# Packing q and k in four pieces with x loaded earlier; in the layers, ScalarE norms the rows and their transposes move behind the k projection

## The chip, the cores and the metric

The kernel runs on one core of a Trainium2 chip. The metric is the device time of one execution in microseconds (us), the median of several runs. Names used below: PE is TensorE, ACT is ScalarE, DVE is VectorE, POOL is GpSimd and SP is the engine that issues the DMAs.

## The reference

Two stages, on 16 sequences of 512 rows with 256 channels, in float32:

```
# stage 1: attention with 16 heads of 16 channels, softmax over the HEADS, then a layernorm
scores = einsum('bqnd,bknd->bnqk', q, k) / sqrt(D)
attn = softmax(scores, axis=1)
x = layernorm(x + (attn @ v) @ Wo.T + bo)
# stage 2: two layers over the same rows
h = shift_token(x)                  # the second half of the channels comes from the row before
q, k = l2norm(q) * qs, l2norm(k) * ks; rotary; local attention with windows of 128 rows, 8 heads of 64
x = x + o @ wo
h = layernorm(shift_token(x)) * lg + lb
a, g = split(h @ w1 + b1)
x = x + (a * gelu(g)) @ w2 + b2
# and a last layernorm(x + ...)
```

## The kernel before

The kernel is written engine by engine: each engine has its own program, in the order of the code, and semaphores join them. Nothing reorders it; an instruction that waits holds back all that stands behind it on its engine.

**Stage 1** (`head_attention`) takes a sequence in 16 units `u` (4 query tiles by 4 key tiles). A unit on PE: subtract the maximum over the heads from the scores `S` (L504), sum the heads' exponentials (L535), the next unit's 16 score matmuls (L494, `scores_bank`), probabilities times v (L521). DVE takes the maximum over the heads (L371) once per unit, so its start times mark the units. Beside this, the projections of the next sequence are spread over the units by `QK_AT`; the float32 q and k are split into three bfloat16 parts (`parts`, ACT L296), and for each of the four pieces (q channels 0 to 127, q 128 to 255, k likewise) the last part is there two units after `READY_AT` = (2, 5, 8, 10), that is at units 4, 7, 10 and 12. SP then copies the parts from 128 partitions into `qk8`, where 8 combinations of parts (`TERMS`) lie in 8 groups of 16 partitions (`pack`, L200). Each transfer writes one group of 16 partitions. Before, q is packed at unit 7 and k at unit 12, 8 transfers of 256 KB each; the first score matmul of the next sequence, at the end of unit 15, waits until both have landed. A loop runs two sequences per round; the first sequence and the last ones are written out. x of the next sequence is loaded (`load_x`) when this one begins, behind its first transposes.

**Stage 2** (`layers`) takes 128 tiles `T` of 128 rows (2 layers, 16 sequences, 4 tiles `w_` each). While tile T is attended, tile T+1 is projected, tile T-1 gets its output projection, tile T-2 its layernorm, and the rows of one or two sequences before go through the feed-forward part. On PE a tile is, in order: transposes of q and k (L1460, L1464), hidden part 0 (L1435), `transpose_h` (x of T+1, L1342, and the normed rows `hn` of T-2, L1346, into the two halves of PSUM bank `X[2]`), times v (L1409), scores (L1380, L1389), transposes of the attention output (L1478), q projection (L1364), output projection (L1487), k projection, transposed probabilities of the first four heads (L1398), hidden part 1, scores of the other heads, times v, v projection, hidden part 2, w2 (L1514), transposed probabilities of the other heads. The w2 matmuls of a tile with even `w_` wait for a product on DVE (`gated`, L839 and L841), which waits for the gelu on ACT (L1095), which ACT does once per two tiles, in the tile with even `w_`, behind the evacuation of the first transposed probabilities (L1129). DVE norms the rows of T-2 at the start of a tile (L1222, L1224), ahead of the low parts of q and k.

Of the kernel before, what the change touches and what calls it, by code (L numbers as in the profile page):

```python
# [682 lines left out]
def layers(nc, ctx, x_a, x_b, y_out, w, W, raw, consts):  # L683
# [322 lines left out]
    def _(act):  # L1006
        def evacuate_hT(T, n, w_, layer):

            act.wait_ge(s_hT, T + 2)
            if tile_exists(T + 1):  # L1010
                p = (w_ + 1) % 2
                nc.scalar.activation(hT0[p][:, HIGH], X[2][:, 0:P], ACT.Copy)
                nc.scalar.activation(hT1[p][:, HIGH, 1:P + 1], X[2][:, P:2 * P], ACT.Copy)

                last_col = zero_col[:] if (w_ + 1) % TILES == TILES - 1 else X[2][:, 2 * P - 1:2 * P]
                last = nc.scalar.activation(hT1[1 - p][:, HIGH, 0:1], last_col, ACT.Copy)
            if tile_exists(T - 2):
                n2, w2_ = back(n, w_, 2)
# [572 lines left out]
```

## Time and profile before

| | us |
|---|---|
| median of 3 runs | 4712.84 (4704.44 to 4716.74) |
| the profiled execution | 4714.33 |
| its span | 4712.5 |
| stage 1, from the start to about | 1700 |
| stage 2, the rest, about | 3010 |
| PE busy in the span | 4314.1 (92%) |
| DVE, ACT, POOL busy | 3282.6 (70%), 2597.2 (55%), 2372.1 (50%) |

The span runs from the first to the last instruction; 1.8 us lie outside it. Busy time of PE says only that a matmul was under way. In stage 1 DVE repeats the same pattern every unit; in stage 2 PE does. The granted clock of PE is 0.97 of full speed on the mean of the span.

### The profile page before, as it was taken

What the parts mean: (1) busy time and instruction counts of PE and PEld (TensorE: products, weight loads), DVE (VectorE), ACT (ScalarE), POOL (GpSimd) and SP (SyncE); (2) the same over time, 40 slices, a digit from 0 to 9 for tenths busy, and PEclk for the clock granted to TensorE, in tenths of its full rate; (3) what the DMA queues carried; (4) which work ended last, traced back from release to release, by engine and by line L of the source; (5) the groups of instructions that cost most, each with busy time, mean ns of one, the idle gap of its engine ahead of it and who ended that gap; (6) DMA issues with size and microseconds to landing.
All of it is one profiled execution on the core that took longest, in us unless ns stands there. A gap on an engine that the chain in (4) does not pass through costs nothing.

```text
span 4712.5 us, 99362 instructions
## 1 busy us (share of the span) xinstructions
PE 4314.1 (92%) x36928; PEld 3584.7 (76%) x36928; DVE 3282.6 (70%) x6004; ACT 2597.2 (55%) x5984; POOL 2372.1 (50%) x1655
## 2 busy tenths in 40 slices
PE   5888888888889869999999999999999999999998
PEld 3666666666666647888888888888888888888887
DVE  3887888888888856666566656656666666666665
ACT  2444444444444436666666666666666666666664
POOL 3887888887888843333333333333333333333332
PEclk8999999999999989999999999999999999999999
DMA  4444334444334310000000000000000000000000
GB/s 84 65 62 64 53 53 58 64 63 64 53 53 57 42 47 22 15 18 15 16 18 15 13 16 17 15 25 15 22 20 20 23 20 22 18 26 20 20 20 25
DMA packets 138238, 160.03 MB, mean 34 GB/s; under 512 B 18079, under 2 KB 103926, under 8 KB 137718
## 3 DMA queue, kind: packets, MB, share of 16 engines
q1 hardware_dynamic: 137718, 153.02, 18.4%
q8 instruction: 336, 5.51, 0.5%
q14 instruction: 184, 1.51, 0.1%
HBM read 52.31 MB, written 25.17 MB: 16 GB/s over the span
## 4 chain that ended last, share of the span: by engine, by line
PE 40%; issue 9%; DVE 8%; ACT 3%; POOL 3%; SPq 0%; DVEq 0%; DMA 0%; POOLq 0%; ACTq 0%
PE b_X L1364 8%; PE b_M L1409 7%; PE b_F L1435 6%; PE b_M L1487 4%; PE b_F L1514 3%; PE b_S L1389 3%; PE b_S L1398 2%; ACT b_p L1123 2%; PE b_S L1380 2%; PE b_M L1478 1%; DVE b_hn L1222 1%; POOL b_rn L955 1%; PE b_X L1346 1%; DVE b_ss L1149 1%; DVE b_mx L1170 1%
## 5 line engine op out<-in xcount | busy, mean ns | idle before, releaser
L319 ACT ACTIVATE a_p<-a_S 128x512 f32<-128x512 f32 x1024 | 529.4, 603 | 700.0 <-PE a_S L504 700.0
L371 DVE TENSOR_REDUCE a_nm<-a_S 128x128 fp32r<-128x2048 f32 x256 | 586.4, 2291 | 228.3 <-PE a_S L494 187.8
L1123 ACT ACTIVATE b_p<-b_S,b_nb,b_rn 128x256 f32<-128x256 f32 (+1 forms) x1024 | 536.7, 534 | 224.2 <-DVE b_nb L1173 223.4
L1364 PE MATMUL b_X<-b_wqkv,b_hT 128*128 128x512 f32 x2304 | 650.4, 418 | 1.4 <-DVE b_hT L1197 1.4
L248 POOL TENSOR_TENSOR a_z<-a_p 128x1024 f32<-128x1024 f32 x256 | 603.7, 2358 | 85.4 <-ACT a_p L319 84.5
L1435 PE MATMUL b_F<-b_hnT,b_w 128*114 128x256 f32 (+1 forms) x4608 | 632.2, 287 | 5.7 <-issue 5.7
L1435 PEld LDWEIGHTS b_F<-b_hnT,b_w 128*114 128x114 f32 (+1 forms) x4608 | 576.7, 178 | 19.2 <-issue 5.9
L948 POOL TENSOR_TENSOR b_t<-b_t 128x512 f32<-128x512 f32 x128 | 165.4, 1292 | 829.7 <-DVE b_t L1147 829.7
L256 POOL TENSOR_TENSOR a_p<-a_p,a_zi 128x640 f32<-128x640 f32 x256 | 397.4, 1552 | 216.4 <-DVE a_zi L397 216.2
L1182 DVE TENSOR_SCALAR b_a<-b_F,w_b 114x256 f32<-114x256 f32 (+1 forms) x384 | 183.7, 478 | 432.6 <-ACT b_g L1044 432.6
L1364 PEld LDWEIGHTS b_X<-b_wqkv,b_hT 128*128 128x128 f32 x2304 | 418.4, 190 | 84.8 <-DVE b_hT L1197 1.8
L1409 PE MATMUL b_M<-b_v,b_PT 128*128 128x64 f32 x3584 | 446.5, 277 | 0.0
L1409 PEld LDWEIGHTS b_M<-b_v,b_PT 128*128 128x128 f32 x3584 | 425.1, 194 | 15.3
L1129 ACT ACTIVATE b_PT<-b_S 128x1024 f32<-128x1024 f32 (+1 forms) x256 | 235.1, 918 | 321.5 <-PE b_S L1398 321.5
L399 DVE TENSOR_TENSOR a_p<-a_p,a_O 128x1408 f32<-128x1408 f32 x256 | 412.1, 1610 | 0.0
L504 PE MATMUL a_S<-a_nm,c_identr 128*128 128x512 f32 x1024 | 316.0, 430 | 92.9 <-DVE a_nm L371 77.0
L494 PE MATMUL a_S<-a_q,a_k 128*128 128x128 bf16 x4096 | 298.1, 226 | 98.0 <-DMA a_k<-a_parts 97.7
L955 POOL TENSOR_TENSOR b_rn<-b_ssc,c_half 128x16 f32<-128x16 f32 x128 | 372.8, 2912 | 21.2 <-DVE b_ssc L1153 16.8
L1514 PE MATMUL b_F<-w_w,b_a 114*128 114x256 f32 (+1 forms) x1536 | 360.1, 384 | 16.4 <-DVE b_a L841 14.7
L504 PEld LDWEIGHTS a_S<-a_nm,c_identr 128*128 128x128 f32 x1024 | 176.1, 190 | 258.0 <-DVE a_nm L371 210.9
L980 POOL TENSOR_TENSOR b_hnT<-b_hnT 128x256 fp32r<-128x256 f32 x128 | 93.8, 733 | 532.4 <-ACT b_hnT L1023 532.4
L996 POOL TENSOR_TENSOR b_rstd<-b_ve,c_half 128x1 f32<-128x1 f32 x128 | 71.0, 555 | 568.8 <-DVE b_ve L1278 568.8
(142 smaller groups left out, 8934.9 us busy)
## 6 DMA issues: line engine op xcount, KB each, us to landing
a_q<-a_parts SPq DMA_DIRECT2D x128, 256.0 KB, 10.1
a_k<-a_parts SPq DMA_DIRECT2D x128, 256.0 KB, 10.7
a_x<-in_x SPq DMA_DIRECT2D x16, 512.0 KB, 15.3
a_xr<-in_x SPq DMA_DIRECT2D x64, 128.0 KB, 3.1
x_after_heads<-a_n SPq DMA_DIRECT2D x64, 128.0 KB, 2.3
b_x<-x_after_heads SPq DMA_DIRECT2D x16, 512.0 KB, 4.1
x_after_layer<-b_xo SPq DMA_DIRECT2D x32, 256.0 KB, 2.3
b_x<-x_after_layer SPq DMA_DIRECT2D x16, 512.0 KB, 3.9
```

The source lines that it names most:

```text
L248: nc.gpsimd.tensor_tensor(z8[:], e[:, 0:8], e[:, 8:16], ALU.add).then_inc(s_zt, 1)
L256: nc.gpsimd.tensor_tensor(e, e, zinv[u % 2][:].unsqueeze(1).to_broadcast([P, HEADS - DVE_HEADS, P]), ALU.mult).then_inc(s_pp, 1)
L319: nc.scalar.activation(probs[u % NE][:, hs], S[:, hs], ACT.Exp, scale=HDIM ** -0.5).then_inc(s_exp, 1)
L371: nc.vector.tensor_reduce(out=negmax[u % 2][:], in_=S[:].rearrange("p h q -> p q h"), axis=AX.X, op=ALU.max, negate=True).then_inc(s_nm, 1)
L399: nc.vector.tensor_tensor(e, e, ZI.unsqueeze(1).to_broadcast([P, DVE_HEADS, P]), ALU.mult).then_inc(s_p, 1)
L504: nc.tensor.matmul(S[:, 4 * b:4 * b + 4], identr[:], negmax[u % 2][:].unsqueeze(1).to_broadcast([P, 4, P]), start=False, stop=True, skip_g ...
L955: nc.gpsimd.tensor_tensor(rn[p][:], ssc[:], half[:], ALU.pow).then_inc(s_rn, 1)
L1123: last = nc.scalar.activation(probs[hf][:, i, keys(w_)], SB[:, i, keys(w_)], ACT.Exp, bias=nb[hf][:, i:i + 1], scale=rn[w_ % 2][:, h:h + 1 ...
L1364: last = nc.tensor.matmul(X[i][:], hT_of(k, a), wqkv[:, b, k, i * INNER:(i + 1) * INNER], start=(k == 0 and (a, b) == PART_PAIRS[0]), stop ...
L1409: last = nc.tensor.matmul(M[:, h * LDIM:(h + 1) * LDIM], PT[hf][:, i, a * P:(a + 1) * P], v[:, w_ if a == w_ % 2 else w_ - 1, h * LDIM:(h ...
L1435: last = nc.tensor.matmul(F[i % 2][0:size, part], w1[:, a, k, col:col + size], hnT[:, b, k, hf * 2 * P:(hf + 1) * 2 * P], start=(k == 0 an ...
L1514: last = nc.tensor.matmul(F[1][:, t], a_sb[h][0:rows, c, t * P:(t + 1) * P], W[layer(-d)]["w2"][0:rows, c], start=(c == 0), stop=(c == CHU ...
```

## The change

Stage 1: `pack` copies one piece (half of q or k, 8 transfers of 128 KB with rows of 1 KB in place of 2 KB) and is called four times, at units 4, 7, 10 and 12; the semaphore of packing is split in two per buffer. x is loaded two sequences ahead of its use, at unit 2, and in the start-up before the first packing. The residual rows (`load_rows`) are issued at other units. The loop has one round less, and four sequence steps in place of two are written out at its end.

Stage 2: the normed rows of T-2 are made by ACT (two instructions, `layernorm`, first in the tile) from rstd and a new shift, which DVE makes with one small instruction. Their transposes on PE move from `transpose_h` to behind the k projection (`transpose_hn`); ACT evacuates them (four instructions, `evacuate_hnT`) behind the first transposed probabilities. The v projection and POOL's low part of `hnT` wait for this.

```
-    PACK_AT = (READY_AT[1] + 2, READY_AT[3] + 2)
+    PACK_AT = tuple(u + 2 for u in READY_AT)
+    X_AT = 2
...
-        with engine.Fori(0, (SEQS - 2) // 2) as i:
+        with engine.Fori(0, (SEQS - 4) // 2) as i:
...
-        def pack(n, par, which):
-            sp.wait_ge(s_part, part_count(n, CT * which + CT - 1, 2))
+        def pack(n, par, i):
+            which, ot = divmod(i, CT)
+            sp.wait_ge(s_part, part_count(n, i, 2))
             for t, (of_k, of_q) in enumerate(TERMS):
                 part = of_k if which else of_q
-                sp.dma_start(qk8[par][which][16 * t:16 * t + 16], parts[which][:, part]).then_inc(s_pack[par], 16)
+                sp.dma_start(qk8[par][which][16 * t:16 * t + 16, :, ot], parts[which][:, part, ot]
+                             ).then_inc(s_pack[par][which], 16)
...
-                if u == 0 and exists(n) and exists(n + 1):
-                    sp.wait_ge(s_pt, 8 * n + CT)
-                    load_x(n + 1)
-                nn, back, uu = lagged(n, u, 3, UNITS)
-                if uu % TILES == TILES - 1 and exists(nn):
-                    load_rows(nn, uu // TILES)
+                if u == X_AT and exists(n) and exists(n + 2):
+                    sp.wait_ge(s_pt, 8 * (n + 1) + CT)
+                    load_x(n + 2)
+                if u % TILES == TILES - 1 and exists(n):
+                    load_rows(n, u // TILES)
...
-                    pool.wait_ge(s_hTe, T + 2)
+                    pool.wait_ge(s_hne, T - 1)
...
+        def evacuate_hnT(T, n, w_, layer):
+            act.wait_ge(s_hnT, T - 1)
+            n2, w2_ = back(n, w_, 2)
+            W2 = W[layer(0 if w_ >= 2 else -1)]
+            need(act, s_hnl, T - 2)
+            for ct in range(CT):
+                for dst in (hnT[:, HIGH, ct, w2_ * P:(w2_ + 1) * P], hnT32[:, ct]):
+                    last = nc.scalar.activation(dst, X[2][:, (2 + ct) * P:(3 + ct) * P], ACT.Identity,
+                                                bias=W2["ln_b"][:, ct:ct + 1], scale=W2["ln_g"][:, ct:ct + 1])
+            last.then_inc(s_hne, 1)
+        def layernorm(t, p, w2_, par2):
+            act.wait_ge(s_lsh, t + 1)
+            need(act, s_hnT, t)
+            for dst, src in ((hn[:, 0:P], x2[par2][:, w2_, 0:P]), (hn[:, P:CH], hs[:, w2_])):
+                last = nc.scalar.activation(dst, src, ACT.Identity, bias=shift[p][:, 0:1], scale=rstd[p][:, 0:1])
+            last.then_inc(s_hn, 1)
...
-                    need(dve, s_hT, T + 1)
-                    nc.vector.tensor_scalar(hn[:, 0:P], x2[p2][:, w2_, 0:P], mv[p][:, 0:1], rstd[p][:, 0:1],
-                                            ALU.subtract, ALU.mult)
-                    nc.vector.tensor_scalar(hn[:, P:CH], hs[:, w2_], mv[p][:, 0:1], rstd[p][:, 0:1],
-                                            ALU.subtract, ALU.mult).then_inc(s_hn, 1)
+                    need(dve, s_hn, T - 3)
+                    nc.vector.tensor_scalar(shift[p][:, 0:1], mv[p][:, 0:1], rstd[p][:, 0:1], -1.0,
+                                            ALU.mult, ALU.mult).then_inc(s_lsh, 1)
...
+        def transpose_hn(T):
+            need(pe, s_hne, T - 2)
+            pe.wait_ge(s_hn, T - 1)
+            for ct in range(CT):
+                last = nc.tensor.transpose(X[2][:, (2 + ct) * P:(3 + ct) * P], hn[:, ct * P:(ct + 1) * P], ident[:])
+            last.then_inc(s_hnT, 1)
...
                 if tile_exists(T + 1):
+                    if tile_exists(T - 2):
+                        pe.wait_ge(s_hne, T - 1)
                     project(2, s_v)
```

Three places of the order. First SP's queue (the DMAs, by destination and source) in the steps of the first sequences. Before:

```order
L200 DMA a_q<-a_parts 16x8x1024 x8
L200 DMA a_k<-a_parts 16x8x1024 x8
L185 DMA a_x<-in_x 128x4x256
L190 DMA a_xr<-in_x 128x256
L200 DMA a_q<-a_parts 16x8x1024 x8
L190 DMA a_xr<-in_x 128x256
L200 DMA a_k<-a_parts 16x8x1024 x8
```

and after the change:

```order
L186 DMA a_x<-in_x 128x4x256
L200 DMA a_q<-a_parts 16x8x512 x16
L200 DMA a_k<-a_parts 16x8x512 x16
L186 DMA a_x<-in_x 128x4x256
L191 DMA a_xr<-in_x 128x256
L200 DMA a_q<-a_parts 16x8x512 x8
L191 DMA a_xr<-in_x 128x256
L200 DMA a_q<-a_parts 16x8x512 x8
L200 DMA a_k<-a_parts 16x8x512 x8
L191 DMA a_xr<-in_x 128x256
L200 DMA a_k<-a_parts 16x8x512 x8
```

Each packing is half as large and there are twice as many; only the last piece of k stands where all of k stood, and a load of x stands ahead of the first packing.

Second, ACT's queue in a tile with even `w_` of stage 2 (`b_hnT` is the transposed normed rows, `b_g` the gate, `b_PT` the transposed probabilities). Before:

```order
L1012 ACTIVATE b_hT<-b_X 128x128
L1013 ACTIVATE b_hT<-b_X 128x128
L1016 ACTIVATE b_hT<-b_X 128x1
L1023 ACTIVATE b_hnT<-b_X,w_b,w_g 128x128 x4
L1081 ACTIVATE b_oT<-b_M 128x512
L1123 ACTIVATE b_p,b_rs<-b_S,b_nb,b_rn 128x128 x4
L1030 ACTIVATE b_sq<-b_X 128x512
L1032 ACTIVATE b_sq<-b_X 128x512
L1129 ACTIVATE b_PT<-b_S 128x4x128
L1095 ACT_TABLE_LOAD
L1095 ACTIVATE b_g<-b_g 114x1280
```

and after:

```order
L1040 ACTIVATE b_hn<-b_x,b_shift,b_rstd 128x128
L1040 ACTIVATE b_hn<-b_hs,b_shift,b_rstd 128x128
L1089 ACTIVATE b_qT<-b_X 128x512
L1091 ACTIVATE b_kT<-b_X 128x4x128
L1060 ACTIVATE b_g<-b_F,w_b 114x256
...
L1048 ACTIVATE b_sq<-b_X 128x512
L1149 ACTIVATE b_PT<-b_S 128x4x128
L1031 ACTIVATE b_hnT<-b_X,w_b,w_g 128x128 x4
L1115 ACT_TABLE_LOAD
L1115 ACTIVATE b_g<-b_g 114x1280
```

The four evacuations now stand between the transposed probabilities and the gelu with its table load, and two new instructions stand ahead of the evacuations of q and k.

Third, PE's queue in such a tile. Before:

```order
L1435 MATMUL b_F<-b_hnT,b_w 114x256 x12
L1342 MATMUL b_X<-c_ident,b_x 128x128 x2
L1346 MATMUL b_X<-c_ident,b_hn 128x128 x2
L1409 MATMUL b_M<-b_v,b_PT 128x64 x8
```

and, at the place to which the two transposes went:

```order
L1506 MATMUL b_M<-w_o,b_oT 128x256 x4
L1383 MATMUL b_X<-b_wqkv,b_hT 128x512 x6
L1365 MATMUL b_X<-c_ident,b_hn 128x128 x2
L1417 MATMUL b_S<-c_ident,b_p 128x128 x4
L1454 MATMUL b_F<-b_hnT,b_w 114x256 x12
```

The transposes of the normed rows left the place between hidden part 0 and times v and now stand ahead of the first transposed probabilities.

## Rows read from the trace of the kernel before

**Rows 1.** Waits by engine and line, 300 to 1600 us: sum, times, longest.

```profile
PE a_S L494 <- DMA a_k<-a_parts: 61.9, 13, 5.0
```

**Rows 2.** Timeline of PE at a sequence's end: start, duration, line, [idle before].

```profile
760.26 1.07 PE L535 MATMUL a_YZ<-a_z,c_ident 128*128 128x128 f32 x8
766.05 1.89 PE L494 MATMUL a_S<-a_q,a_k 128*128 128x128 bf16 x16 [4.72 <-DMA a_k<-a_parts]
```

**Rows 3.** Timeline of DVE, line 371, around two sequence boundaries.

```profile
756.89 2.28 DVE L371 TENSOR_REDUCE a_nm<-a_S 128x128 fp32r<-128x2048 f32 x1
...
769.35 2.29 DVE L371 TENSOR_REDUCE a_nm<-a_S 128x128 fp32r<-128x2048 f32 x1 [6.67 <-issue]
...
777.96 2.29 DVE L371 TENSOR_REDUCE a_nm<-a_S 128x128 fp32r<-128x2048 f32 x1 [3.39 <-PE a_S L494]
...
794.56 2.29 DVE L371 TENSOR_REDUCE a_nm<-a_S 128x128 fp32r<-128x2048 f32 x1 [0.31 <-PE a_S L494]
...
800.73 2.29 DVE L371 TENSOR_REDUCE a_nm<-a_S 128x128 fp32r<-128x2048 f32 x1 [0.59 <-PE a_S L494]
...
851.87 2.29 DVE L371 TENSOR_REDUCE a_nm<-a_S 128x128 fp32r<-128x2048 f32 x1 [0.18 <-PE a_S L494]
...
857.82 2.28 DVE L371 TENSOR_REDUCE a_nm<-a_S 128x128 fp32r<-128x2048 f32 x1
...
869.08 2.29 DVE L371 TENSOR_REDUCE a_nm<-a_S 128x128 fp32r<-128x2048 f32 x1 [5.47 <-PE a_S L494]
...
876.83 2.29 DVE L371 TENSOR_REDUCE a_nm<-a_S 128x128 fp32r<-128x2048 f32 x1 [0.59 <-PE a_S L494]
```

**Rows 4.** Timeline of SP's DMA issues: the packing of k.

```profile
746.24 5.21 SPq L200 DMA_DIRECT2D a_k<-a_parts  x8
```

**Rows 5.** Timeline of ACT: the last part of k's first and second piece.

```profile
735.59 0.68 ACT L296 ACTIVATE a_parts<-a_B,a_bk 128x512 bf16<-128x512 f32 x1
...
745.52 0.69 ACT L296 ACTIVATE a_parts<-a_B,a_bk 128x512 bf16<-128x512 f32 x1 [1.33 <-PE a_B L462]
```

**Rows 6.** Busy time by stretch: five engines, PE clock, DMA share, GB/s.

```profile
756.00:760.00 4.00, 4.00 (x48) 3.08 (x48) 3.97 (x6) 0.63 (x2) 3.92 (x4) 1.00 1.07 118
...
2000.00:3300.00 1300.00, 1262.67 (x8978) 1109.07 (x8977) 806.88 (x1854) 824.38 (x2024) 433.80 (x336) 0.99 0.06 17
```

**Rows 7.** DMA view, 754 to 764 us, packing: packets, MB, engine share.

```profile
q1 hardware_dynamic: 648, 1.19, 107.4%
```

**Rows 8.** DMA view, 1746.5 to 1752 us, a load in 1 KB packets.

```profile
q1 hardware_dynamic: 590, 0.53, 31.8%
```

**Rows 9.** Waits, 2000 to 4500 us: PE's matmuls on the normed rows.

```profile
PE b_X L1346 <- DVE b_hn L1224: 45.3, 54, 5.2
```

**Rows 10.** Timelines of ACT, DVE, PE in a tile with even `w_`.

```profile
3789.42 1.03 ACT L1129 ACTIVATE b_PT<-b_S 128x1024 f32<-128x1024 f32 x1 [0.28 <-PE b_S L1398]
3790.47 1.28 ACT L1095 ACT_TABLE_LOAD   x1
...
3793.73 0.48 DVE L1182 TENSOR_SCALAR b_a<-b_F,w_b 114x256 f32<-114x256 f32 x1 [0.26 <-ACT b_g L1044]
...
3796.36 0.28 DVE L841 TENSOR_TENSOR b_a<-b_a,b_g 112x128 f32<-112x128 f32 x1
...
3796.81 2.82 PE L1514 MATMUL b_F<-w_w,b_a 114*128 114x256 f32 x12
```

**Rows 11.** Timelines of ACT and DVE, second layer, a tile with `w_` 0.

```profile
3747.45 0.46 ACT L1044 ACTIVATE b_g<-b_F,w_b 114x256 f32<-114x256 f32 x1
...
3748.44 0.47 DVE L1182 TENSOR_SCALAR b_a<-b_F,w_b 114x256 f32<-114x256 f32 x1
```

**Rows 12.** Timelines of ACT, DVE, PE in a tile with odd `w_`.

```profile
3801.98 1.57 DVE L1222 TENSOR_SCALAR b_hn<-b_x,b_mv,b_rstd 128x128 f32<-128x128 f32 x1 [0.20 <-POOL b_rstd L996]
...
3804.01 0.44 PE L1346 MATMUL b_X<-c_ident,b_hn 128*128 128x128 f32 x2 [1.00 <-DVE b_hn L1224]
...
3804.87 1.52 ACT L1023 ACTIVATE b_hnT<-b_X,w_b,w_g 128x128 fp32r<-128x128 f32 x4
```

More of the change, by code:

```diff
@@ L110, in head_attention @@
     s_vv = sem("v_evacuated")
-    s_pack = [sem(f"packed{i}") for i in range(2)]
+    s_pack = [[sem(f"packed_{n}{i}") for n in "qk"] for i in range(2)]
     s_S = sem("scores")
@@ L149, in sequences @@
         one(0, 0, 0)
-        with engine.Fori(0, (SEQS - 2) // 2) as i:
+        with engine.Fori(0, (SEQS - 4) // 2) as i:
             one(2 * i + 1, 1, i)
             one(2 * i + 2, 0, i + 1)
-        one(SEQS - 1, 1, SEQS // 2 - 1)
-        one(SEQS, 0, SEQS // 2)
+        for n in range(SEQS - 3, SEQS + 1):
+            one(n, n % 2, n // 2)
     def part_count(n, i, part):
@@ L488, in scores_bank @@
             if u == 0 and b == 0:
-                pe.wait_ge(s_pack[par], PACKED * (r + 1))
+                for of in s_pack[par]:
+                    pe.wait_ge(of, PACKED * (r + 1))
             qt, kt = u // TILES, u % TILES
@@ L737, in layers @@
     stats = sb("stats", [P, 2, 6])
-    mv, ve, rstd = ([sb(f"{n}{i}", [P, 2]) for i in range(2)] for n in ("mv", "ve", "rstd"))
+    mv, ve, rstd, shift = ([sb(f"{n}{i}", [P, 2]) for i in range(2)] for n in ("mv", "ve", "rstd", "shift"))
     hn = sb("hn", [P, CH])
@@ L761, in layers @@
     s_hTe = sem("hT_evacuated")
+    s_hnT = sem("hnT")
+    s_hne = sem("hnT_evacuated")
     s_hTl = sem("hT_low")
@@ L793, in layers @@
     s_rs = sem("ln_rstd")
+    s_lsh = sem("ln_shift")
     s_hn = sem("ln_normed")
@@ L1009, in evacuate_hT @@
             act.wait_ge(s_hT, T + 2)
[L1010 to L1018, printed above, removed]
-                W2 = W[layer(0 if w_ >= 2 else -1)]
-                need(act, s_hnl, T - 2)
-                for ct in range(CT):
-                    for dst in (hnT[:, HIGH, ct, w2_ * P:(w2_ + 1) * P], hnT32[:, ct]):
-                        last = nc.scalar.activation(dst, X[2][:, (2 + ct) * P:(3 + ct) * P], ACT.Identity,
-                                                    bias=W2["ln_b"][:, ct:ct + 1], scale=W2["ln_g"][:, ct:ct + 1])
-            last.then_inc(s_hTe, 1)
+            p = (w_ + 1) % 2
+            nc.scalar.activation(hT0[p][:, HIGH], X[2][:, 0:P], ACT.Copy)
+            nc.scalar.activation(hT1[p][:, HIGH, 1:P + 1], X[2][:, P:2 * P], ACT.Copy)
+            last_col = zero_col[:] if (w_ + 1) % TILES == TILES - 1 else X[2][:, 2 * P - 1:2 * P]
+            nc.scalar.activation(hT1[1 - p][:, HIGH, 0:1], last_col, ACT.Copy).then_inc(s_hTe, 1)
+        def evacuate_hnT(T, n, w_, layer):
[14 more added lines that the diff above has]
+            last.then_inc(s_hn, 1)
         def squares(t):
@@ L1068, in one @@
                 live, feed = tile_exists(T), seq_exists(n - 1)
+                if tile_exists(T - 2):
+                    layernorm(T - 2, p, (w_ - 2) % TILES, par if w_ >= 2 else 1 - par)
                 if live:
@@ L1088, in one @@
                     evacuate_PT(w_, 0)
+                if tile_exists(T - 2):
+                    evacuate_hnT(T, n, w_, layer)
                 if w_ % 2 == 0:
@@ L1334, in transpose_h @@
                 pe.wait_ge(s_hTe, T + 1)
-            if tile_exists(T + 1):
-                wn = (w_ + 1) % TILES
-                pn = par if w_ < TILES - 1 else 1 - par
-                if wn == 0:
-                    pe.wait_ge(s_x[pn], x_count(n + 1, pn))
-                for ct in range(CT):
-                    last = nc.tensor.transpose(X[2][:, ct * P:(ct + 1) * P], x_tok[pn][:, wn, ct * P:(ct + 1) * P], ident[:])
-            if tile_exists(T - 2):
-                pe.wait_ge(s_hn, T - 1)
-                for ct in range(CT):
-                    last = nc.tensor.transpose(X[2][:, (2 + ct) * P:(3 + ct) * P], hn[:, ct * P:(ct + 1) * P], ident[:])
-            last.then_inc(s_hT, 1)
+            wn = (w_ + 1) % TILES
+            pn = par if w_ < TILES - 1 else 1 - par
+            if wn == 0:
+                pe.wait_ge(s_x[pn], x_count(n + 1, pn))
+            for ct in range(CT):
+                last = nc.tensor.transpose(X[2][:, ct * P:(ct + 1) * P], x_tok[pn][:, wn, ct * P:(ct + 1) * P], ident[:])
+            last.then_inc(s_hT, 1)
+        def transpose_hn(T):
+            need(pe, s_hne, T - 2)
+            pe.wait_ge(s_hn, T - 1)
+            for ct in range(CT):
+                last = nc.tensor.transpose(X[2][:, (2 + ct) * P:(3 + ct) * P], hn[:, ct * P:(ct + 1) * P], ident[:])
+            last.then_inc(s_hnT, 1)
         counts = {}
```

15 lines of the change are left out of this document (9 added, 6 removed).

## The prediction, made before the changed kernel was run

> **What bounds the kernel now.** I read the busy time by stretch, then the waits of each stage, then the timelines of all engines at the two places that the change touches.
>
> Stage 1 is set by a cycle through DVE's maximum over the heads: one row per unit, and in undisturbed units the next start follows by a fixed step. The reader is to see two such steps in [rows 3]: unit 14 takes 857.82 - 851.87 = 5.95 us, and a unit with a residual takes 800.73 - 794.56 = 6.17 us. At a sequence boundary this breaks. From unit 15 to unit 1 of the next sequence it takes 876.83 - 857.82 = 19.01 us where 5.95 + 6.17 = 12.12 us would do: 6.9 us lost. Where the loop turns as well it is 777.96 - 756.89 = 21.07 us: 8.95 lost. The cause stands in PE's timeline: it finishes its last work at 760.26 + 1.07 = 761.33 and the first score matmuls start at 766.05, behind the packed k [rows 2]; then they take 1.89 us for 16. The waits of the stage name the same transfer 13 times with 61.9 us in 1300 us [rows 1]. The rest of the 6.9 us is the empty pipeline filling again.
>
> Stage 2 is set by PE, which is under way for 1262.67 of 1300 us [rows 6]. Its largest wait is for the normed rows, 45.3 us in 54 tiles of the 108 in that window [rows 9]. It is the tiles with odd `w_`: there DVE's first norming instruction takes 1.57 us and PE stands 1.00 us [rows 12]. A second place is as tight without showing as a wait: in a tile with even `w_` PE starts w2 at 3796.81, 0.17 us after the product on DVE ends (3796.36 + 0.28 = 3796.64) [rows 10]. That product hangs on the gelu, and the gelu on ACT's evacuation of the transposed probabilities.
>
> **Stage 1, term by term.** When would the last piece land after the change? The packing of k was issued at 746.24 [rows 4] and released PE at 766.05 [rows 2]: 19.8 us for 8 transfers of 256 KB, 2.10 MB. At 118 GB/s [rows 6] that is 17.8 us of moving and 2.0 us around it. The first piece of k can now start when its last part is written, at 735.59 + 0.68 = 736.3 [rows 5], and takes 8.9 + 2.0: landed at 747.2. The second starts, as k did, at 746.2 and lands at 746.2 + 2.0 + 8.9 = 757.1, or 0.5 us later if it queues behind the first. PE wants it at 761.3: 4 us to spare. The doubled count of transfers (32 per sequence) costs SP 5.21 us per eight [rows 4] and SP has nothing else to do there. The load of x no longer stands behind the packing and has a whole sequence of time. So the wait goes.
>
> The unknown in this is what a 1 KB packet costs. Bounds: nothing less than half of a 2 KB one, and at most the same. Over packing, 648 packets in 10 us at a share of 107.4% of 16 engines are 16 x 10 x 1.074 / 648 = 0.265 us each [rows 7]; in a load, mostly of 1 KB packets, to all 128 partitions, 16 x 5.5 x 0.318 / 590 = 0.047 us [rows 8]. So a packet as such costs at most 0.05 us, and the other 0.2 us of the packing is the 2 KB going into 16 partitions. Half the bytes should take half of it. I take bytes, ratio 0.5 to 0.6. The two pieces of k have 761.3 - 736.3 - 2.0 = 23.0 us where both took 17.8 at ratio 0.5, so the wait stays away up to a ratio of 0.5 x 23.0 / 17.8 = 0.65.
>
> Concerning the destination: the page "SBUF — State Buffer" of the Trainium skill (Door 1, the DMA port swizzle) says that DMA bandwidth goes by how many of the 16 ports the partitions reach; by its table 16 neighbouring partitions reach four of them, an estimate of a quarter of 435 GB/s, 109 GB/s. By that rule bytes are what counts, and the 118 GB/s above agree roughly. That rule raises my chance for the gain and changes no term.
>
> There are 15 boundaries. Before, 6 of them are turns of the loop and 9 are not; after, 5 and 10. A plain one gives back 6.9 us. A turn costs 21.07 - 19.01 = 2.06 us more than a plain boundary now, with part of it hidden in the stall; I leave 3 us of it standing (bounds 2 to 5), so a turn gives 5.95, and the one that is no longer a turn gives 8.95. Sum: 9 x 6.9 + 5 x 5.95 + 8.95 = 62.1 + 29.8 + 9.0 = **-101 us**. Bounds: -85 with 5 us and a little lost in unit 1, -113 with every boundary undisturbed. The start-up, where packing can begin a piece earlier but behind one more load of x, may give a few us more and is left out of the sum.
>
> **Stage 2, term by term.** ACT's four evacuations take 1.52 us as a group [rows 12], 1.42 us of added queue, since neighbours overlap by about 0.1 (probabilities 3789.42 + 1.03 against the table load at 3790.47 shows no gap to put them in [rows 10]). In a tile with even `w_` they now stand ahead of the table load and the gelu. DVE waits for the gate behind that gelu (0.26 us idle at 3793.73), so value, row maximum, product and PE's w2 all move by 1.42; with 0.04 us of the 0.17 as slack, PE gets **+1.38 us**. What they left, the place between hT and oT, gives nothing in these tiles: ACT waited for PE there. In the second layer at `w_` 0 the gate ends at 3747.91 and DVE takes the value only at 3748.44, busy with the final statistics [rows 11]: 0.5 us of cover, so +0.9. With 64 such tiles, 16 of this kind: 48 x 1.38 + 16 x 0.9 = **+81 us**. Bounds: nothing, if PE had other slack before w2, and 64 x 1.5 = +96.
>
> In a tile with odd `w_` there is no gelu, and what follows the evacuations has room. The wait for the normed rows ahead of times v goes; it was 45.3 / 54 = 0.84 us per odd tile. DVE is freed of 1.57 us and a shorter one, but ACT gets two instructions of about 0.38 us ahead of the evacuations of q and k, behind a further handover POOL to DVE to ACT. PE's next need, the attention output normed by DVE, then comes about 0.5 us earlier, not 0.84: I take 0.5 x 64 = **-32 us**. Bounds 0 and -54. The two transposes themselves only change place. In even tiles DVE's norming was hidden and ACT's two instructions are as well, because times v and the mask matmuls stand ahead of PE's need for q and k.
>
> Also moved, and costed at nothing: POOL waits for the evacuated `hnT` first in its tile, so the rotations and the norms behind it are done up to 2.6 us later; they are needed at the end of the tile for DVE's scaling of k, and of k's transposes PE has the time of w2 and the probabilities, about 4 us, in front. If that cover goes, DVE's statistics and rstd follow late, and then ACT's new first instructions.
>
> Sum: -101 + 81 - 32 = **-52 us**. The profiled execution took 4714.3 us (span 4712.5 and 1.8 outside), 1.5 us above the median of the runs shown, so 4714.3 - 52 = 4662, against the median 4661. I predict **4661 us**.
>
> **The rivals.**
> 1. Smaller transfers don't land earlier. If each transfer costs a fixed time, eight take 19.8 us whatever their size: the eight transfers of [rows 4] cost 2.5 us each, and that is also what a fixed price would look like. Then the first piece of k lands at 756.1, the second at 775.9, and PE waits 14.6 us instead of 4.7: 15 x 9.9 = +148, with stage 2's +49 some 4910 us. It decides from a packet ratio of 0.65 on; at a ratio of 0.8 the pieces take 28.5 us, PE waits 5.5 us as now, and the time is 4713 + 49 + 12 = 4774. Against it: the engines' share is 1.07 throughout [rows 6], so there are always packets under way, and [rows 8]. The rule that speaks for it is in "DMA: Bandwidth & Descriptors" of the Trainium skill (Rules for kernel authors): coalesce small transfers into one large one, since each pays about 2 us. By its formula of 2.0 us and bytes over 436 GB/s, as an estimate, a half-size transfer would still take 2.3 of 2.6 us. Chance 0.08, slower.
> 2. ACT's detour is not on the path. If gelu is not what PE waits for, stage 2 gives -32 and the time is 4712.8 - 101 - 32 = 4580. For it: PE shows no idle time before w2. Against: 0.17 us between two engines is what a handover takes, and the same tiles show DVE waiting for ACT. Chance 0.10, faster.
> 3. ACT's and POOL's detours cost twice: DVE comes late for scaling k or for rstd as well, another 1.4 us in each even tile, 64 x 1.4 = +90, and the odd tiles give nothing back (+32): 4661 + 122 = 4783; with half of it 4722. For it: POOL's three instructions stand right behind the new wait. Chance 0.08, half of it within 0.3%.
> 4. The forecast, 0.74: its own range is 4630 to 4695 (stage 1 -85 to -113, stage 2 +20 to +75).
>
> **How the numbers follow.** A measurement of this kernel can tell some 0.3%, 14 us, from no change; that is 4699 at the fast side. Faster: the forecast, rival 2 and a small part of rival 3, 0.84. Same: 0.05. Slower: rival 1 and the rest of rival 3, 0.11. The range takes in the forecast's own range and half of rival 2 below, and leaves rival 1 and most of rival 3 out: 4600 to 4705.
>
> **What would show it.** Stage 1 right: no wait of PE's score matmuls for the packed k, DVE's step from unit 15 to unit 1 at about 12 us, the packing of a piece 10 to 11 us from its first issue to its landing, the stage about 100 us shorter. Stage 2 right: in tiles with even `w_` an idle time of 1.2 to 1.5 us ahead of PE's w2, released by DVE's product, and no more waits for the normed rows; the stage about 50 us longer. The prediction is wrong if packets of 1 KB take over 0.17 us while packing, if w2 starts without a wait, or if the loop turns cost more than 5 us each once the stall that covers them is gone.

## The result, and the profile of the changed kernel

| | before | changed |
|---|---|---|
| median, us (4 runs each, same chip) | 4710.6 | 4638.1 |
| range, us | 4704.4 to 4716.7 | 4631.8 to 4642.0 |
| profiled span, us | 4712.5 | 4639.7 |
| mean granted clock of PE | 0.973 | 0.983 |

The ratio is 0.9845, interval 0.9826 to 0.9864: 1.55% faster, 73 us by ratio and span. Forecast was 4661 us in a range of 4600 to 4705.

I split both traces at DVE's last maximum over the heads (the 256th start of its line, the end of stage 1's cycle). It starts at 1661.6 us before and at 1535.9 after: **stage 1 is 125.8 us shorter**. From there to the span's end it is 3050.9 before and 3103.8 after: **stage 2 is 52.9 us longer**. In the traces of the experiments the layers of before take 3050.9 to 3058.2 us and the changed ones 3103.8 to 3116.2, so the second number is known to some 10 us.

**Stage 1.** The timeline of DVE's head maximum at a plain boundary (units 15, 0, 1) and at one where the loop turns, in the changed kernel, beside [rows 3]:

```profile
799.02 2.28 DVE L373 TENSOR_REDUCE a_nm<-a_S 128x128 fp32r<-128x2048 f32 x1
804.73 2.28 DVE L373 TENSOR_REDUCE a_nm<-a_S 128x128 fp32r<-128x2048 f32 x1
810.51 2.29 DVE L373 TENSOR_REDUCE a_nm<-a_S 128x128 fp32r<-128x2048 f32 x1 [0.59 <-PE a_S L497]
...
890.16 2.28 DVE L373 TENSOR_REDUCE a_nm<-a_S 128x128 fp32r<-128x2048 f32 x1
896.77 2.29 DVE L373 TENSOR_REDUCE a_nm<-a_S 128x128 fp32r<-128x2048 f32 x1 [0.82 <-issue]
907.54 2.29 DVE L373 TENSOR_REDUCE a_nm<-a_S 128x128 fp32r<-128x2048 f32 x1 [5.57 <-PE a_S L497]
```

A plain boundary takes 810.51 - 799.02 = 11.49 us where 19.01 were needed; a turn still takes 17.38. The last piece of k for the first of them, as SP's timeline shows its issue, and DMA activity by stretch (last columns: PE clock, DMA share, GB/s):

```profile
788.37 5.09 SPq L200 DMA_DIRECT2D a_k<-a_parts  x8
```

```profile
789.00:797.00 8.00, 7.40 (x77) 5.61 (x76) 7.75 (x9) 3.12 (x7) 7.14 (x6) 1.00 1.00 128
797.00:799.00 2.00, 2.00 (x45) 1.83 (x47) 1.97 (x6) 1.01 (x3) 2.00 (x2) 1.00 0.80 147
799.00:800.00 1.00, 1.00 (x23) 0.75 (x12) 1.00 (x2) 0.38 (x1) 1.00 (x1) 1.00 0.02 7
```

The DMA engines fall silent at about 799, 10.6 us after the first issue, and PE's first score matmuls with this k start at 803.29. No wait for the packed k is left in the loop; the one that stays is that of the start-up.

There is more in the boundary than the wait. Busy time by stretch in the trace of before, at the plain boundary at 857.82 of [rows 3], with PE's timeline:

```profile
864.00:868.00 4.00, 0.94 (x10) 0.94 (x11) 0.00 (x0) 0.00 (x0) 2.48 (x2) 0.77 1.01 224
868.00:872.00 4.00, 4.00 (x44) 3.00 (x43) 2.29 (x1) 0.00 (x0) 0.00 (x0) 0.50 0.02 6
...
872.00:876.00 4.00, 3.41 (x22) 2.63 (x21) 2.77 (x4) 2.54 (x5) 1.21 (x1) 0.87 0.01 2
```

```profile
867.06 1.89 PE L494 MATMUL a_S<-a_q,a_k 128*128 128x128 bf16 x16 [4.72 <-DMA a_k<-a_parts]
868.88 1.94 PE L521 MATMUL a_O<-a_p,a_v 128*32 128x128 f32 x32
...
876.62 1.08 PE L521 MATMUL a_O<-a_p,a_v 128*32 128x128 f32 x32
```

After PE had stood 4.72 us, its granted clock was at 0.50, the 1.2 GHz level, and the same 32 matmuls took 1.94 us in place of 1.08. With the wait gone, the clock shows 1.00 from 804 to 808 in the changed kernel. At a turn it still falls. PE's timeline and a stretch of the changed kernel, at the turn of 890.16:

```profile
900.15 0.96 PE L507 MATMUL a_S<-a_nm,c_identr 128*128 128x512 f32 x3 [2.32 <-issue]
903.20 0.79 PE L507 MATMUL a_S<-a_nm,c_identr 128*128 128x512 f32 x1 [2.08 <-issue]
```

```profile
902.00:906.00 4.00, 2.80 (x14) 2.72 (x15) 0.00 (x0) 1.34 (x3) 1.37 (x2) 0.50 0.01 4
```

Here PE stands twice by issue, that is, for nothing that the profile's semaphores show, and then runs at the lower level. All five turns of the changed kernel have these two idle times, of 1.8 to 2.3 us; at the other four the profile puts the first down to DVE's maximum, which is itself 0.8 to 1.1 us late by issue. Packets of instructions pass through the DMA engines and stand in the trace: one of 16 KB from the queue `q8` ends 1.3 to 1.7 us before PE resumes, at each of these ten idle times. So what PE waits for at a turn looks to be its next instructions.

**Stage 2.** PE's waits from 2000 to 4500 us (sum, times, longest), beside [rows 9]:

```profile
PE b_F L1537 <- DVE b_a L847: 67.2, 53, 1.5
PE b_S L1408 <- DVE b_kT L1184: 25.3, 35, 5.3
PE b_M L1497 <- DVE b_o_n L1252: 9.9, 38, 0.3
```

The 45.3 us for the normed rows are gone and w2 waits instead; over the whole stage it is 87.1 us in 65 tiles, median 1.22, when the rows of PE's timeline are added up; the page's group of this line has nearly the same, and below it stands that of the kernel before:

```profile
L1537 PE MATMUL b_F<-w_w,b_a 114*128 114x256 f32 (+1 forms) x1536 | 363.8, 387 | 86.5 <-DVE b_a L847 85.9
L1514 PE MATMUL b_F<-w_w,b_a 114*128 114x256 f32 (+1 forms) x1536 | 360.1, 384 | 16.4 <-DVE b_a L841 14.7 <-DVE b_xo L1285 0.6
```

So 14.7 us of this wait stood already before: about 0.59 us in each of the second layer's tiles with `w_` 0, and two long ones at the end of the stage. The change added some 70 us to it.

Timelines of ACT, DVE and PE in one of them, beside [rows 10]:

```profile
3793.29 1.03 ACT L1149 ACTIVATE b_PT<-b_S 128x1024 f32<-128x1024 f32 x1 [0.49 <-PE b_S L1417]
3794.21 1.50 ACT L1031 ACTIVATE b_hnT<-b_X,w_b,w_g 128x128 fp32r<-128x128 f32 x4
3795.72 1.28 ACT L1115 ACT_TABLE_LOAD   x1
...
3798.99 0.48 DVE L1202 TENSOR_SCALAR b_a<-b_F,w_b 114x256 f32<-114x256 f32 x1 [1.21 <-ACT b_g L1060]
...
3801.58 0.28 DVE L847 TENSOR_TENSOR b_a<-b_a,b_g 112x128 f32<-112x128 f32 x1
...
3802.00 2.85 PE L1537 MATMUL b_F<-w_w,b_a 114*128 114x256 f32 x12 [1.17 <-DVE b_a L847]
```

The table load starts 3795.72 - 3794.21 = 1.51 us later behind the probabilities than it could, DVE then waits 1.21 for the gate, and PE's w2 1.17 for the product.

What a tile gained or lost can be read from the periods between the starts of w2 in neighbouring tiles, changed kernel less before, over the first 120 of them:

| tile | median, us | sum, us |
|---|---|---|
| `w_` 0 | +1.35 in the first layer, +0.89 in the second | +33.2 |
| `w_` 2 | +1.33 | +38.7 |
| `w_` 1 | -0.1 | -3.2 |
| `w_` 3 | -0.61 in the first layer, -0.90 in the second | -22.9 |

The even tiles lose 72 us and the odd ones gain 26, nearly all of it with `w_` 3. With `w_` 1, 24.9 us of waits for the normed rows went, and 16.9 us for the scaled k (L1408) and 7.4 us for the normed attention output (L1497) came in their place; both lines stand in the view of the waits above.

### The profile page after: what moved, and what is told of

Same layout as the page of the kernel before. It is cut to its first block, busy times and chain, and to the rows that moved or that the text cites. A ratio compares the mean times of both kernels' runs of the same rounds, so it can differ in the third digit from the quotient of the medians.

```text
span 4639.7 us, 99525 instructions
## 1 busy us (share of the span) xinstructions
PE 4267.8 (92%) x36868; PEld 3557.7 (77%) x36928; DVE 3230.3 (70%) x5876; ACT 2664.9 (57%) x6240; POOL 2357.0 (51%) x1655
## 3 DMA queue, kind: packets, MB, share of 16 engines
q1 hardware_dynamic: 174582, 153.04, 17.8%
## 4 chain that ended last, share of the span: by engine, by line
PE 29%; issue 15%; ACT 9%; DVE 8%; POOL 4%; SPq 0%; ACTq 0%; DMA 0%; DVEq 0%; POOLq 0%
PE b_X L1383 8%; PE b_M L1506 4%; PE b_F L1454 3%; PE b_M L1428 3%; PE b_F L1537 3%; PE b_S L1417 3%; ACT b_hnT L1031 2%; ACT b_p L1143 2%; POOL b_rn L961 2%; PE b_S L1408 2%; PE b_M L1497 1%; DVE b_mx L1190 1%; DVE b_a L1202 1%; ACT L1115 1%; ACT b_g L1115 1%
## 5 line engine op out<-in xcount | busy, mean ns | idle before, releaser
L1537 PEld LDWEIGHTS b_F<-w_w,b_a 114*128 114x128 f32 (+1 forms) x1536 | 284.8, 192 | 135.4 <-issue 68.0
L253 POOL TENSOR_TENSOR a_z<-a_z 128x512 f32<-128x512 f32 x256 | 327.7, 1280 | 22.9 <-POOL a_z L250 5.7
L538 PEld LDWEIGHTS a_YZ<-a_z,c_ident 128*128 128x128 f32 x2048 | 256.3, 194 | 78.3 <-POOL a_z L253 52.8
```

Of the source, the lines that this page charges most:

```text
L1537: last = nc.tensor.matmul(F[1][:, t], a_sb[h][0:rows, c, t * P:(t + 1) * P], W[layer(-d)]["w2"][0:rows, c], start=(c == 0), stop=(c == CHU ...
```

## The experiments

Edits are against the kernel that is named. "Before" in the ratios is the kernel before, run on the same chip.

**1. The two halves apart** (`s1_only`, `s2_only`). The diff was divided at the functions: `head_attention` (stage 1) of one kernel with `layers` (stage 2) of the other.

> Stage 1 of the changed kernel with the layers of the kernel before. The two traces put 125.8 us of gain ahead of the last maximum over the heads and 52.9 us of loss behind it. If the two halves are independent: 126 us faster than before, 4585 us (4575 to 4595), ratio 0.973. Rival: part of the loss in stage 2 comes from stage 1 (something in the layers started late or the clock fell because PE waited less in stage 1); then the gain is smaller, 73 to 110 us, and the layers take longer than the 3050.9 us that they take before.

> Stage 1 of the kernel before with the changed layers. Independent halves: 53 us slower than before, 4764 us (4753 to 4775), ratio 1.011, with PE standing 1.2 us ahead of w2 in 65 tiles as in the changed kernel. Rival: the layers' loss depends on the changed stage 1; then the time is within 15 us of before.

Measured: `s1_only` 4595.2 us, ratio 0.974 (0.9723 to 0.9757), 123 us faster; `s2_only` 4776.0, ratio 1.0124 (1.0107 to 1.0141), 58 us slower. The sum, -64, stands to the -73 of both together as their intervals allow; 4776.0 lies 1 us outside the range that was expected. Within these intervals the halves are independent, and `s2_only` shows the same wait ahead of w2: 69.5 us in 53 tiles. The layers of `s1_only` take 3058.0 us, inside the spread of that stage.

**2. The transfers halved, nothing else** (`half_old`, against before):

```
-                sp.dma_start(qk8[par][which][16 * t:16 * t + 16], parts[which][:, part]).then_inc(s_pack[par], 16)
+                for ot in range(CT):
+                    sp.dma_start(qk8[par][which][16 * t:16 * t + 16, :, ot], parts[which][:, part, ot]
+                                 ).then_inc(s_pack[par], 16)
```

> The kernel before, with each packing transfer issued as two of half the size, at the same place in the program. Bytes theory (my prediction): the same bytes into the same 16 partitions take the same time, and the packed k releases PE at most 1 to 2 us later for the eight added issues of 0.65 us each, partly hidden behind the moving: within 25 us of before, 4710 to 4735. Fixed price per transfer or per packet (rival 1): the eight transfers of k become sixteen at up to 2.5 us each, k lands up to 20 us later at each of the 15 boundaries, the ones of q too: up to 4710 + 15 x 20 = 5010 us; a packet ratio of 0.8 in place of 0.5 gives 4710 + 15 x 10.7 = 4870 us.

Measured: 4726.1 us, ratio 1.0018 (1.0008 to 1.0028), 8.5 us slower. PE's waits from 300 to 1600 us, beside [rows 1]:

```profile
PE a_S L496 <- DMA a_k<-a_parts: 82.9, 13, 6.8
```

The packed k comes 82.9 / 13 - 61.9 / 13 = 1.6 us later for eight transfers more, as expected. In this queue a transfer's price is its bytes; what each transfer adds by itself is 0.2 us.

**3. The parts of stage 1** (`pieces_only`, `rest_only`, against before). The first takes only the packing:

```
-    PACK_AT = (READY_AT[1] + 2, READY_AT[3] + 2)
+    PACK_AT = tuple(u + 2 for u in READY_AT)
...
-            sp.wait_ge(s_part, part_count(n, CT * which + CT - 1, 2))
+            which, ot = divmod(i, CT)
+            sp.wait_ge(s_part, part_count(n, i, 2))
```

> The kernel before with the packing by pieces alone; loads of x, loads of rows, loop and layers as before. Theory: nearly all of stage 1's gain comes from k landing before PE wants it. The boundaries gave (19.0 - 11.5) x 9 plain ones and about 4 us at each of 6 turns, 68 + 24 = 92 us: 4713 - 92 = 4621 us (4610 to 4640). Rival: the gain also needs x to be ahead of the packing in the queue; then the load of x, which stands behind the packing as before, makes PE wait for the next sequence's rows, and less than half is gained, over 4665 us.

The second takes all else of stage 1 and packs as before:

```
-        with engine.Fori(0, (SEQS - 2) // 2) as i:
+        with engine.Fori(0, (SEQS - 4) // 2) as i:
...
-                if u == 0 and exists(n) and exists(n + 1):
-                    sp.wait_ge(s_pt, 8 * n + CT)
-                    load_x(n + 1)
+                if u == X_AT and exists(n) and exists(n + 2):
+                    sp.wait_ge(s_pt, 8 * (n + 1) + CT)
+                    load_x(n + 2)
```

> The kernel before with x loaded a sequence ahead, the rows' loads issued at their new units and the loop one turn shorter, but the packing in two transfers as before; layers as before. If the parts of stage 1 add up, this gives what packing by pieces doesn't: 126 - 92 = 34 us faster, 4679 us (4670 to 4700): the start-up's 8.6 us, the 15.6 us of stalls in unit 11 of even sequences, and the turn that is gone. If these stalls come from the packing's transfers and not from loads or loop, the gain is 10 us or less, 4700 to 4715.

Measured: `pieces_only` 4599.6 us, ratio 0.9756 (0.9742 to 0.9771), 115 us faster; `rest_only` 4715.3, ratio 0.9997 (0.9988 to 1.0007). Packing by pieces is nearly the whole gain. Both theories miss: `pieces_only` lies 10 us under its range and `rest_only` 15 us above, because the start-up and the stalls in unit 11, which I had given to the rest, came with the pieces; the second half of the expectation for `rest_only` is met. From the starts of DVE's head maximum, in us:

| | first start | 15 boundaries (unit 15 to 1), sum | excess in unit 11 | last start |
|---|---|---|---|---|
| before | 67.8 | 299.7 | 15.5 | 1661.6 |
| `rest_only` | 68.0 | 298.3 | 12.4 | 1656.2 |
| `half_old` | 68.1 | 319.6 | 0 | 1667.1 |
| `pieces_only` | 59.3 | 206.2 | 0 | 1542.7 |
| changed | 59.2 | 200.2 | 0 | 1535.9 |

Of the last 7 us between `pieces_only` and the changed kernel, 6 lie in the boundaries: the sixth turn of the loop. The start-up's 8.6 us come from the pieces too, not from x. The excess in unit 11 is the time that this unit takes over 5.53 us, a stall that I had not read: before, in seven sequences (all at one half of the loop's body), this unit took 7.1 to 9.0 us in place of 5.53. PE's timeline of before in one of them:

```profile
731.90 0.42 PE L521 MATMUL a_O<-a_p,a_v 128*32 128x128 f32 x7
734.32 0.95 PE L521 MATMUL a_O<-a_p,a_v 128*32 128x128 f32 x25 [2.00 <-issue]
```

PE stops in the middle of one group, by issue, while q is being packed. `half_old` packs the same bytes in the same units and does not have it. The DMA view of narrow windows shows where the packets of instructions fall: before, none from 723 to 729 us and one from 730 to 733; in `half_old`, in the same sequence, one from 726 to 730:

```profile
q8 instruction: 1, 0.02, 3.9%
```

```profile
q8 instruction: 1, 0.02, 2.9%
```

Counted from the start of the maximum in unit 7, this 16 KB packet starts at 21.2 to 21.6 us in all seven stalled sequences of before, ends at 23.1 to 23.4 and PE stops at 23.1. In `half_old` it starts at 14.7 to 15.2 us in these sequences and in the changed kernel at 14.1 to 14.5, and PE has what it needs. So the stall is a late packet of instructions; that it is late because it stands behind the packing's transfers fits, but what holds it in the queue isn't shown.

**4. ACT's order** (`ahead_q`, against the changed kernel). The transposes stand ahead of the q projection, the evacuations behind those of `oT`:

```
                     projection_ready(T + 1, layer(0 if w_ < 3 else 1))
+                if tile_exists(T - 2):
+                    transpose_hn(T)
+                if tile_exists(T + 1):
                     project(0, s_q)
...
                     nc.scalar.activation(oT[:], M[:], ACT.Copy).then_inc(s_oTe, 1)
+                if tile_exists(T - 2):
+                    evacuate_hnT(T, n, w_, layer)
```

with both taken away at their old places.

> The changed kernel, with the two transposes of the normed rows on PE moved from behind the k projection to ahead of the q projection, and their four evacuations on ACT from behind the first transposed probabilities to behind the transposed attention output. There ACT stood idle for 0.3 us and the transposes of the probabilities have some 1.5 us to spare, so the 1.14 us that the first probabilities come later is hidden. Theory: the w2 wait of the changed layers (87 us over 65 tiles) comes from the four evacuations ahead of the gelu; it goes and nothing takes its place: 4638 - 87 = 4551 us (4545 to 4580), 3.4% under the kernel before. Rival A: the w2 wait has another cause in the changed layers (norming on ACT, the later low part on POOL): 4630 to 4645. Rival B: the cost moves to the first transposed probabilities, PE waits up to 1.1 us there in each of 128 tiles: 4551 + 64 to 140, 4615 to 4690.

Measured: 4549.5 us, ratio 0.9649 (0.9636 to 0.9662). That is 0.0196 of 4713, **92 us** under the changed kernel (88 by the two profiled spans), with the expected 4551 met. In part by luck: of the 87 us only 71 went, since 15 us of the wait stood before the change and stay; the even tiles' periods are 77 us shorter than in the changed kernel, and the rest isn't accounted for. ACT's timeline in a tile with even `w_`, and PE's waits from 2000 to 4400 us:

```profile
3721.79 0.60 ACT L1099 ACTIVATE b_oT<-b_M 128x512 f32<-128x512 f32 x1 [2.61 <-PE b_M L1497]
3722.28 1.50 ACT L1031 ACTIVATE b_hnT<-b_X,w_b,w_g 128x128 fp32r<-128x128 f32 x4
...
3727.40 1.03 ACT L1149 ACTIVATE b_PT<-b_S 128x1024 f32<-128x1024 f32 x1 [0.28 <-PE b_S L1417]
3728.45 1.28 ACT L1115 ACT_TABLE_LOAD   x1
```

```profile
PE b_F L1538 <- DVE b_a L847: 7.1, 13, 0.6
```

The same four instructions take the same 1.50 us, but now the probabilities behind them have time to spare: PE transposes them without a wait, and the table load follows the evacuated probabilities at once.

**5. The other way round** (`behind_gate`, against the changed kernel): PE as it was, ACT's `evacuate_hnT(T, n, w_, layer)` moved from ahead of the gelu to behind `gate(T, 1, w_, layer)`.

> The changed kernel, with the four evacuations on ACT behind the second gate in place of ahead of the gelu. PE's projection of v waits for these evacuations (it writes their bank), and in tiles with even w_ they would end at 1.1 us after it wants to start. Theory: the wait ahead of w2 goes and one of about 1.1 us ahead of the v projection takes its place in the same 64 tiles, 1.22 - 1.1 = 0.1 us gained in each: 4638 - 8 = 4630 us (4620 to 4650). Rival: the v projection is not held, or the hold is absorbed by the wait for the product: then up to 87 us are gained, 4551 us.

Measured: 4766.3 us, ratio 1.0113 (1.0097 to 1.0128): both theories miss by over 100 us. Timelines of PE, DVE and GpSimd in a tile with even `w_`, and PE's clock by stretch:

```profile
3789.07 2.78 PE L1383 MATMUL b_X<-b_wqkv,b_hT 128*128 128x512 f32 x6 [1.05 <-ACT b_hnT L1031]
...
3795.90 0.69 DVE L1177 TENSOR_TENSOR b_t<-b_t,b_rn 128x512 f32<-128x512 f32 x1 [1.18 <-POOL b_rn L961]
...
3789.09 0.73 POOL L986 TENSOR_TENSOR b_hnT<-b_hnT 128x256 fp32r<-128x256 f32 x1 [16.94 <-ACT b_hnT L1031]
3789.78 1.93 POOL L954 TENSOR_TENSOR b_t<-b_t 128x512 f32<-128x512 f32 x1
3791.67 1.33 POOL L956 TENSOR_TENSOR b_t<-b_t 128x512 f32<-128x512 f32 x1
3792.95 2.91 POOL L961 TENSOR_TENSOR b_rn<-b_ssc,c_half 128x16 f32<-128x16 f32 x1
```

```profile
3790.00:3791.00 1.00, 1.00 (x4) 0.81 (x3) 1.00 (x2) 0.99 (x4) 1.00 (x1) 0.50 0.00 0
```

The wait ahead of w2 is gone (6.9 us in three tiles), with PE's order as it was, so it hung on ACT's order alone. The expected wait is there (1.05 us ahead of the v projection), and two costs with it. PE runs at 0.50 behind it in this tile: six matmuls take 2.78 us that take 1.66 at full clock. It does so in part of the tiles only: of the 31 with a wait of 1.05 to 1.07 us, 15 show over 2 us for these matmuls and 16 show 1.66. And GpSimd, which waits for the evacuations first in its tile, ends the norms at 3795.86, for which DVE waits 1.18 us.

**6. GpSimd's order** (`bg_pool` against `behind_gate`, `after_pool` against the changed kernel): GpSimd's low part of the normed rows, with its wait, moved behind the rotations and norms:

```
-                if tile_exists(T - 2):
-                    ...
-                    pool.wait_ge(s_hne, T - 1)
-                    nc.gpsimd.tensor_tensor(hnT[:, LOW, :, cols], hnT32[:], hnT[:, HIGH, :, cols], ALU.subtract
                 if tile_exists(T + 1):
                     rotate(T + 1)
                 if tile_exists(T + 1):
                     norms(T + 1, (w_ + 1) % 2)
+                if tile_exists(T - 2):
+                    ...
```

> The kernel behind_gate (4766 us) with the same move on GpSimd. There the evacuations come later still, and DVE waited 1.18 us for the norms in a tile whose rotations GpSimd started 4 us late. PE stood 1.05 us ahead of the v projection and then ran 3.2 us at a granted clock of 0.5, which costs some 1.3 us per tile. If the norms are the cause of the loss: GpSimd's wait goes and the time falls to 4640 to 4690. If PE's gap and the lower clock are: at most 0.6 us per pair of tiles comes back, 64 x 0.6 = 38 us, 4728 to 4766.

> The changed kernel, with GpSimd's low part of the normed rows moved from first in its tile to behind the rotations and the norms, so that they no longer wait behind it for ACT's evacuations. My prediction costed that wait at nothing; if that is right, the time stays that of the changed kernel, 4638 us (4628 to 4648), and all of the 87 us ahead of w2 belongs to ACT's order. Rival 3 of the prediction in a small form: part of the loss in stage 2 comes through GpSimd (the norms late, then DVE's scaling of k and the scores behind it, which wait 28 us in the trace); then 10 to 40 us are gained, 4600 to 4628.

Measured: `bg_pool` 4670.2 us, ratio 0.9899 (0.9873 to 0.9926), 101 us (0.0214 of 4713) better than `behind_gate`: most of that loss came through GpSimd, and the theory that PE's gap and clock were the larger part (4728 to 4766) fell. What is left against `after_pool`, 34 us, goes with the held v projection (76.2 us in 53 tiles) and the clock behind it, less the w2 wait. `after_pool` 4635.4, ratio 0.9827 (0.981 to 0.9843): its interval overlaps that of the changed kernel, and 4635.4 lies in the range expected if the wait costs nothing. In the changed kernel the same wait costs nothing that can be measured (the two ratios are 8 us apart, within their intervals).

**7. The turns of the loop** (`unroll4`, `flat`, against `ahead_q`): stage 1's loop with four sequences in its body, and no loop.

```
-        with engine.Fori(0, (SEQS - 4) // 2) as i:
-            one(2 * i + 1, 1, i)
-            one(2 * i + 2, 0, i + 1)
-        for n in range(SEQS - 3, SEQS + 1):
+        for n in range(1, SEQS + 1):
```

> The kernel ahead_q (4549 us) with four sequences instead of two in the body of stage 1's loop: 2 turns instead of 5. In its trace a turn takes 17.0 us from the start of unit 15 to that of unit 1 where a plain boundary takes 11.5 us: each turn 5.5 us. If it is the turn itself: 4549 - 3 x 5.5 = 4533 us (4528 to 4540). If the time belongs to something that comes every second sequence whatever the loop: 4549.

> The kernel ahead_q (4549 us) with stage 1 written out in full, no loop and no turns. If it is the turn itself: 4549 - 5 x 5.5 = 4522 us (4515 to 4532). Rival: code that runs once is fetched at a cost of its own, which shows as idle time by issue in each sequence; then the gain is less or gone, 4530 to 4560.

Measured: `unroll4` 4539.9 us, ratio 0.9627 (0.961 to 0.9643); `flat` 4517.2, ratio 0.9577 (0.9561 to 0.9593), **4.2% under the kernel before**, the fastest here. The intervals put `flat` 34 us under `ahead_q`, and do not tell `unroll4` from it; its trace does: the 15 boundaries take 184.0 us, 15.5 less, and the two that turn 17.3 and 17.8. In `flat` all take 11.3 us (170.0), and PE's waits by issue at the head maximum's line are gone. Its units take 5.50 us against 5.53 in the loop. Of the gain 6.7 us are lost again at the start-up: the first maximum starts at 64.8 us, in `ahead_q` at 58.1. The theory that the turn itself costs the time holds, and the rival, that code which runs once pays as much, does not.

## Why the prediction came out as it did

**The boundaries: right in sum, wrong at the turns.** They were to give 101 us. They give 299.7 - 200.2 = 99.5. Two terms in it were off and cancel, which is luck. A plain boundary gives 19.0 - 11.5 = 7.5 us, not 6.9, since the undisturbed steps are 5.71 and 5.78 and not the 5.95 and 6.17 that I took from units 14 and 4. A turn leaves 17.1 - 11.5 = 5.6 us standing where I took 3 and bounded at 5. By the last of its own signs (a turn over 5 us) the prediction is wrong there.

**The wait's cause: right; what lies behind it: misread.** Of the 7.5 us at a plain boundary the wait is 4.7, and 2.8 come behind it. I put these down to the empty pipeline filling again. The stretches show the granted clock at 0.50 behind the wait, and two groups of matmuls alone take (1.89 - 1.11) + (1.94 - 1.08) = 1.6 us longer by it. The 1.89 us for 16 score matmuls that I quoted were the sign: undisturbed they take 1.11. The sum did not need the cause; the turns did, since there the clock still falls after the change.

**Left out of stage 1: 24 us.** The start-up, named and not costed, gave 8.6 us; the stall in unit 11 gave 15.5. Its row stood in the trace: PE's idle time by issue under the packing of q. I had read only the boundaries. This is what makes the stage -126 and not -101.

**The packets: right.** The piece lands 10.6 us after its first issue, against 10.9 worked out, and 4.3 us ahead of PE, against 4. Rival 1 is refuted by `half_old`. The Trainium skill's page "SBUF — State Buffer" (Door 1) sets a transfer's rate by the ports that its partitions reach, so that half the bytes into the same 16 partitions cost half; the 0.2 us per added transfer agree. The Trainium skill's page "DMA: Bandwidth & Descriptors" (Anatomy of one DMA) has a fixed 2.0 us for each DMA issued from GpSimd; here, issued from SP and one behind the other in a queue, the transfers do not show such a price: the 2.0 us that the prediction worked out around the moving stand once for all eight.

**Stage 2, even tiles: right.** Predicted +1.38 us in each, +0.9 in those of the second layer with `w_` 0, and +81 in all. The periods show 1.33 to 1.35 and 0.89 in the median and 72 us in sum; against `ahead_q`, which takes the cost away, the same tiles are 77 us longer, and the two kernels' ratios give 92. Over eleven sequences of the first layer the even tiles are 1.47 and 1.30 us longer on the mean than those of `ahead_q`, and the odd ones equal to 0.03. Rival 2 falls with that. For it I wrote that PE shows no idle time before w2; that was misread, since the second layer's tiles with `w_` 0 show 0.59 us. They are the ones to which I gave 0.5 us of cover, and that size was right.

**Stage 2, odd tiles: near in sum, wrong in shape.** Predicted -0.5 us in each of 64 tiles, -32. The periods give -26: -0.6 to -0.9 with `w_` 3 and -0.1 with `w_` 1, where waits for the attention output and the scaled k took the place of the one that went. `ahead_q` is 0.0091 of 4713, 43 us, under `s1_only`, but that is not the odd tiles alone: their periods are 29 us shorter, and PE's waits by issue at the transposes of q and k are 19.1 us in `s1_only` and 5.4 in `ahead_q`. So +72 - 26 = +46 stands for the +81 - 32 = +49 of the text; the ratio of `s2_only` gives 58, the profiled pair 53 for the whole stage.

**GpSimd's cover: right, and thinner than it read.** The wait costed at nothing costs nothing that can be measured (`after_pool`). But in `behind_gate`, where the evacuations end some 3 us later behind the transposed probabilities in even tiles and 1 us later in odd ones, the same wait costs 101 us. Rival 3 had its mechanism right, and this kernel lies less than those 1 to 3 us from it.

The centre was 23 us high: the 24 us left out of stage 1, with the smaller errors about even.

## What to carry to other kernels

An instruction that is moved on an in-order engine costs what it delays, not what it takes: the same 1.50 us of evacuations cost some 80 to 90 us ahead of a gelu, and behind the attention output the even tiles are as long as they were before the change. So before a move, list for each candidate place which result stands behind it and how long its reader can wait. When a stall goes, look at the clock around it and at waits by issue elsewhere in the same loop too: 15.5 of the 126 us here lay in a place that no wait on a semaphore named. And read the loop's turns once the stalls that covered them are gone; here they were worth another 34 us.

## What the runs showed of the hardware

- Behind an idle time of PE of 4.7 us, and behind two of 2.1 to 2.3 us, the granted clock was at 0.50, in the first case for some 7 us (an estimate from means of 0.77, 0.50 and 0.87 over three stretches of 4 us). In `behind_gate` it was at 0.50 behind a single idle time of 1.05 us, for 3.4 us (from means of 0.63, 0.50, 0.50 and 0.83 over 1, 1, 1 and 2 us), in about half of such tiles. Behind the 1.17 us ahead of w2 in the changed kernel it stayed at 1.00, and w2 took 2.85 us, where tiles without a wait show 2.75 to 2.86. What tells these waits of about 1.1 us apart was not tried.
- A turn of stage 1's loop costs 5.6 us: DVE starts 0.8 to 1.1 us late by issue, PE stands twice for 1.8 to 2.3 us, each time until 1.3 to 1.7 us after the end of a 16 KB packet of instructions, and then comes the lower clock. Code without the loop has none of it and runs each unit 0.03 us faster; its first maximum started 6.7 us later.
- PE can stall 2 us by issue in mid-group while eight transfers of 256 KB are under way; with sixteen of 128 KB in the same place, or with pieces, it does not. The packet of instructions started 21.2 to 21.6 us behind a fixed point of the sequence in the stalled cases and 13.9 to 15.2 us in the others.
